# Attention on one Trainium2 core: the engine loops run over pairs of query blocks, and the q rows stand in a ring of two blocks

## The reference

```python
q = (x @ Wq.T).reshape(N, S, H, hd).transpose(0, 2, 1, 3)   # k, v alike; N 4, S 2048, H 16, hd 32
energy = jnp.einsum('nhqd,nhkd->nhqk', q, k)
attn = jax.nn.softmax(energy / jnp.sqrt(hd), axis=3)
out = jnp.einsum('nhql,nhld->nhqd', attn, v)
x = _layernorm(x + out.transpose(0, 2, 1, 3).reshape(N, S, D))
y = clip(einsum('bsi,oi->bso', x, sign(weights)) * scale + bias, -100, 100)
x = _layernorm(x + y)
```

## Time and profile before

| | us |
|---|---|
| median of 3 runs (lowest to highest) | 3060.59 (3056.12 to 3070.12) |
| the profiled execution | 3055.99 |
| its span | 3053.8 |
| PE busy / DVE busy / ACT busy in the span | 2816.3 / 2320.8 / 2300.6 |
| idle time of PE ahead of its score matmuls (line 637) | 194.4 |
| ACT_TABLE_LOAD in attention (line 764) | 16 of 1.283 each |

### The profile page before, as it was taken

The page is one execution under the profiler, slowest core; times in us unless marked ns, Lnnn a source line. Parts: engine busy times, 40 slices in busy tenths (PEclk is TensorE's granted clock), DMA queues, the critical chain, the costliest instruction groups (busy, mean ns, idle before and its releaser), DMA issues.

```text
span 3053.8 us, 79127 instructions
## 1 busy us (share of the span) xinstructions
PE 2816.3 (92%) x29276; PEld 1339.6 (44%) x29276; DVE 2320.8 (76%) x2050; ACT 2300.6 (75%) x2789; POOL 342.5 (11%) x342
## 2 busy tenths in 40 slices
PE   8999999898989889898989889898988989997998
PEld 7888888632323223232323223332322323335887
DVE  4443344398979788887979788887978888896998
ACT  4333333398979788887979788997978888894665
POOL 0000000100000000000000000000000000003665
PEclk9999999899999999999999999999999999997999
DMA  5454544457666575656666584756657565655563
GB/s 197 169 188 165 181 176 175 170 124 155 128 140 131 122 162 111 141 112 148 127 136 137 115 168 106 154 121 143 133 121 159 114 146 112 148 114 161 205 205 128
DMA packets 223651, 446.51 MB, mean 146 GB/s; under 512 B 15442, under 2 KB 130130, under 8 KB 198868
## 3 DMA queue, kind: packets, MB, share of 16 engines
q0 software_dynamic: 27504, 200.29, 33.9%
q1 hardware_dynamic: 186596, 224.71, 23.6%
q10 hardware_dynamic: 9216, 16.78, 1.4%
HBM read 123.47 MB, written 117.96 MB: 79 GB/s over the span
## 4 chain that ended last, share of the span: by engine, by line
PE 60%; issue 11%; ACT 5%; DVE 2%; ACTq 0%; DMA 0%; POOL 0%; DVEq 0%; SPq 0%; POOLq 0%
PE banks L637 27%; PE banks L666 24%; PE banks L1008 6%; ACT probs L764 5%; PE banks L683 1%; DVE partial L818 1%; DVE partial L821 1%; PE banks L997 1%; PE banks L990 1%; PE banks L1004 0%; DMA total<-partial 0%; POOL score_rows L587 0%; PE banks L991 0%; ACTq L756 0%; ACT y L1026 0%
## 5 line engine op out<-in xcount | busy, mean ns | idle before, releaser
L764 ACT ACTIVATE probs<-banks 128x1024 f32<-128x1024 f32 x2048 | 1892.6, 1162 | 154.5 <-PE banks L637 153.0
L637 PE MATMUL banks<-score_rows 97*32 97x512 f16 x16384 | 1170.2, 392 | 194.4 <-ACT probs L764 111.8
L666 PE MATMUL banks<-probs,v_keys 128*32 128x512 f32 x8192 | 1093.3, 610 | 5.8 <-ACT probs L764 4.5
L637 PEld LDWEIGHTS banks<-score_rows 97*32 97x32 f16 x16384 | 379.8, 97 | 1243.6 <-ACT probs L764 681.9
L821 DVE TENSOR_TENSOR partial<-partial,probs 128x2048 f32<-128x2048 f32 x384 | 879.6, 2291 | 19.0 <-ACT probs L764 6.4
L818 DVE TENSOR_TENSOR partial<-probs 128x2048 f32<-128x2048 f32 x192 | 440.1, 2292 | 163.4 <-ACT probs L764 160.6
L606 POOL DMA_DIRECT2D total<-partial x191 | 164.5, 861 | 1986.6 <-DVE partial L821 1030.2
L666 PEld LDWEIGHTS banks<-probs,v_keys 128*32 128x32 f32 x8192 | 253.0, 114 | 234.6 <-issue 29.3
L821 DVE TENSOR_TENSOR total<-total,probs 128x2048 f32<-128x2048 f32 x128 | 292.7, 2287 | 10.6 <-ACT probs L764 8.5
L348 DVE TENSOR_TENSOR qk_lo<-banks,qk_hi 128x512 f16<-128x512 f32 x128 | 88.5, 691 | 239.2 <-ACT qk_hi L292 239.2
L818 DVE TENSOR_TENSOR total<-probs 128x2048 f32<-128x2048 f32 x64 | 146.4, 2288 | 140.6 <-ACT probs L764 136.5
(11 more groups left out here) (94 smaller groups left out, 2159.1 us busy)
## 6 DMA issues: line engine op xcount, KB each, us to landing
total<-partial POOLq DMA_DIRECT2D x191, 1024.0 KB, 8.0
x_in<-in_L_attn_x SPq DMA_DIRECT2D x17, 1024.0 KB, 7.3
scratch_q_raw<-qk_raw SPq DMA_DIRECT2D x16, 1024.0 KB, 5.5
scratch_k_raw<-qk_raw SPq DMA_DIRECT2D x16, 1024.0 KB, 5.6
scratch_v<-v_out SPq DMA_DIRECT2D x16, 1024.0 KB, 5.0
score_rows<-scratch_q_hi SPq DMA_DIRECT2D x128, 128.0 KB, 6.4
score_rows<-scratch_k_hi SPq DMA_DIRECT2D x128, 128.0 KB, 3.8
v_keys<-scratch_v SPq DMA_DIRECT2D x64, 256.0 KB, 5.5
```

Of the source, the lines that this page charges most:

```text
L637: last = nc.tensor.matmul(scores_of(unit)[part, i, :], k_rows[:, h, keys], q_rows[:, h, qb * BLK:(qb + 1) * BLK], start=True, stop=True)
L666: last = nc.tensor.matmul(banks[rows, out_bank(qb), :], v_keys[:, kt, rows], probs[:, kt % P_RING, h, :], start=(kt == 0), stop=(kt == KT ...
L764: nc.scalar.activation(probs[:, kt % P_RING, heads, :], scores_of(qb * UNITS + u), ACT.Exp, scale=SCALE / GAIN ** 2).then_inc(a_prob, 1)
```

## The change

The loops of PE, ACT and DVE run over 32 pairs of query blocks, not over 16 items, and write out two blocks (`par` is 0 or 1), not four. The last pair is written out behind PE's loop, and the first ahead of DVE's. `score_rows` is split into `q_pair`, two blocks of q, and `k_item`, an item's k. Block n of q goes to slot n % 2, and SP loads block n+2 when the scores of block n are done. Since 64 units don't divide by 3 slots, the last unit of a pair takes slot 1, and the credit of `a_prob` is 4. SP increments `a_order` ahead of some DMAs.

```diff
-    rows16 = sb("score_rows", [P, 2, G, S], FP16)
-    q_rows, k_rows = rows16[0:KROWS, 0], rows16[0:KROWS, 1]
+    q_pair = sb("q_pair", [P, 2 * G * BLK], FP16)
+    k_item = sb("k_item", [P, G * S], FP16)
+    q_rows = q_pair[0:KROWS].rearrange("p (b h t) -> p b h t", b=2, h=G)
+    k_rows = k_item[0:KROWS].rearrange("p (h t) -> p h t", h=G)
...
+    PAIRS = ITEMS * QB // 2
+    LAST_PAIR = PAIRS - 1
+    CREDIT = SLOTS + 1
+
+    def slot_of(unit):
+
+        return 1 if unit == 2 * UNITS - 1 else unit % SLOTS
 
     def scores_of(unit):
 
-        return banks[:, 2 * (unit % SLOTS):2 * (unit % SLOTS) + 2, :]
+        return banks[:, 2 * slot_of(unit):2 * slot_of(unit) + 2, :]
...
-            for c in range(1, QB):
-                load_q(0, c)
+            load_q(0, 1)
             with sp.Fori(0, LAST) as it:
...
                     sp.wait_ge(a_score, st * UNITS + UNITS)
-                    load_q(ahead, qb)
+                    sp.sem_inc(a_order, 1)
+                    load_q(it if qb < 2 else ahead, (qb + 2) % QB)
...
+            for qb in range(2):
+                sp.wait_ge(a_score, (LAST * QB + qb + 1) * UNITS)
+                load_q(LAST, qb + 2)
...
-        def fast_scores(it, qb, kt):
+        def fast_scores(pair, par, kt):
             if kt == 0:
-                pe.wait_ge(a_q[qb], it * FIRST_Q + FIRST_Q)
-            if qb == 0 and kt % TPB == 0:
-                pe.wait_ge(a_k[kt // TPB], it * FIRST_K + FIRST_K)
+                pe.wait_ge(a_q[par], pair * FIRST_Q + FIRST_Q)
+            if par == 0 and kt % TPB == 0:
+                pe.wait_ge(a_k[kt // TPB], pair // 2 * FIRST_K + FIRST_K)
             for half in range(2):
-                unit = qb * UNITS + 2 * kt + half
-
-                pe.wait_ge(a_prob, it * ITEM_UNITS + slot_before(unit) + 1 + SLOTS)
+                unit = par * UNITS + 2 * kt + half
+
+                pe.wait_ge(a_prob, pair * 2 * UNITS + slot_before(unit) + 1 + CREDIT)
...
-        def item(scores, it):
-
-            steps(scores, it, 0, range(HEAD, KT))
-            for qb in range(1, QB):
-                steps(scores, it, qb, range(KT))
-            if it is not LAST:
-                steps(scores, it + 1, 0, range(HEAD))
-            denominators(it, QB - 1)
+        def two_blocks(scores, pair):
+
+            steps(scores, pair, 0, range(HEAD, KT))
+            steps(scores, pair, 1, range(KT))
+            if pair is not LAST_PAIR:
+                steps(scores, pair + 1, 0, range(HEAD))
+            denominators(pair, 1)
...
-            with pe.Fori(0, ITEMS - 1) as it:
-                item(scores, it)
-            item(scores, LAST)
+            with pe.Fori(0, LAST_PAIR) as pair:
+                two_blocks(scores, pair)
+            two_blocks(scores, LAST_PAIR)
...
-        def item(it):
-            for qb in range(QB):
-                st = it * QB + qb
+        with act.Fori(0, PAIRS) as pair:
+            for par in range(2):
+                st = pair * 2 + par
...
-        nc.vector.tensor_scalar(q_rows[3 * HD:KROWS], k_rows[3 * HD:KROWS], 0.0, shift[3 * HD:KROWS], ALU.mult, ALU.add).then_inc(a_shift, 1)
+        nc.vector.tensor_scalar(q_pair[3 * HD:KROWS], k_item[3 * HD:KROWS, 0:2 * G * BLK], 0.0, shift[3 * HD:KROWS],
+                                ALU.mult, ALU.add).then_inc(a_shift, 1)
...
-        item(0, True)
-        with dve.Fori(1, ITEMS) as it:
-            item(it, False)
+        two_blocks(0, True)
+        with dve.Fori(1, PAIRS) as pair:
+            two_blocks(pair, False)
```

More of the change, by code:

```diff
@@ L406, in attend @@
     out_sb, den_sb = wf_scaled[:, 0:2, :], wf_scaled[:, 2:4, :]
-    a_q = [sem(f"a_q{c}") for c in range(QB)]
+    a_q = [sem(f"a_q{c}") for c in range(2)]
     a_k = [sem(f"a_k{c}") for c in range(QB)]
@@ L438, in attend @@
     UNITS = 2 * KT
-    ITEM_UNITS = QB * UNITS
+    PAIRS = ITEMS * QB // 2
     LAST = ITEMS - 1
+    LAST_PAIR = PAIRS - 1
     HEAD = DEN_TILE + 1
@@ L443, in attend, with out_bank @@
     FIRST_K = 48
+    CREDIT = SLOTS + 1
+    def slot_of(unit):
+        return 1 if unit == 2 * UNITS - 1 else unit % SLOTS
     def scores_of(unit):
-        return banks[:, 2 * (unit % SLOTS):2 * (unit % SLOTS) + 2, :]
+        return banks[:, 2 * slot_of(unit):2 * slot_of(unit) + 2, :]
     def slot_before(unit):
-        return unit - SLOTS if unit >= SLOTS else max(v for v in range(ITEM_UNITS) if v % SLOTS == unit) - ITEM_UNITS
-    def out_bank(qb):
-        return 2 * SLOTS + qb % 2
+        units = range(2 * UNITS)
+        return max(v for v in [*[u - 2 * UNITS for u in units], *range(unit)] if slot_of(v % (2 * UNITS)) == slot_of(unit))
+    def out_bank(par):
+        return 2 * SLOTS + par
     v_src = dram["v"].rearrange("(n b) (t p) (g d) -> n g b p t d", n=N, p=P, g=NG)
@@ L636, in fast_scores, with exact_scores @@
                         keys = slice(kt * P + HD * c, kt * P + HD * c + HD)
-                        last = nc.tensor.matmul(scores_of(unit)[part, i, :], k_rows[:, h, keys],
-                                                q_rows[:, h, qb * BLK:(qb + 1) * BLK], start=True, stop=True)
+                        last = nc.tensor.matmul(scores_of(unit)[part, i, :], k_rows[:, h, keys], q_rows[:, par, h, :],
+                                                start=True, stop=True)
                 last.then_inc(a_score, 1)
-        def exact_scores(it, qb, kt):
-            st = it * QB + qb
+        def exact_scores(pair, par, kt):
+            st = pair * 2 + par
             if kt == 0:
@@ L655, in exact_scores, with values @@
                 last.then_inc(a_score, 1)
[L657 to L661, removed]
+        def values(pair, par, kt):
+            st = pair * 2 + par
+            if par == 0 and kt % TPB == 0:
+                pe.wait_ge(a_v[kt // TPB], pair // 2 * 16 + 16)
+            pe.wait_ge(a_prob, st * UNITS + 2 * kt + 2 + CREDIT)
             if kt == 0:
@@ L665, in values, with denominators @@
                 rows = slice(HD * h, HD * h + HD)
-                last = nc.tensor.matmul(banks[rows, out_bank(qb), :], v_keys[:, kt, rows], probs[:, kt % P_RING, h, :],
+                last = nc.tensor.matmul(banks[rows, out_bank(par), :], v_keys[:, kt, rows], probs[:, kt % P_RING, h, :],
                                         start=(kt == 0), stop=(kt == KT - 1))
             last.then_inc(a_pv, 1)
[L670 to L673, removed]
+        def denominators(pair, par):
+            st = pair * 2 + par
+            parts = [total[:, par]]
+            if pair is LAST_PAIR and par == 1:
                 pe.wait_ge(a_merged, (st + 2) * (GROUPS - 1) - 1)
@@ L682, in denominators, with steps, all_blocks @@
                     rows = slice(HD * h, HD * h + HD)
-                    last = nc.tensor.matmul(banks[rows, out_bank(qb), :], ones[:], part[:, h, :],
+                    last = nc.tensor.matmul(banks[rows, out_bank(par), :], ones[:], part[:, h, :],
                                             start=(part is parts[0]), stop=(part is parts[-1]))
             last.then_inc(a_den, 1)
-        def steps(scores, it, qb, tiles):
+        def steps(scores, pair, par, tiles):
             for kt in tiles:
                 if kt + LAG < KT:
[L691 to L699, removed]
-        def item(scores, it):
-            steps(scores, it, 0, range(HEAD, KT))
-            for qb in range(1, QB):
-                steps(scores, it, qb, range(KT))
-            if it is not LAST:
-                steps(scores, it + 1, 0, range(HEAD))
-            denominators(it, QB - 1)
-        def all_items(scores):
+                    scores(pair, par, kt + LAG)
+                elif par == 0:
+                    scores(pair, 1, kt + LAG - KT)
+                elif pair is not LAST_PAIR:
+                    scores(pair + 1, 0, kt + LAG - KT)
+                values(pair, par, kt)
+                if kt == DEN_TILE and par == 1:
+                    denominators(pair, 0)
+        def two_blocks(scores, pair):
[4 more added lines that the diff above has]
+            denominators(pair, 1)
+        def all_blocks(scores):
             for kt in range(LAG):
@@ L736, in _ @@
             pe.wait_ge(m_ones, 1)
-            all_items(exact_scores)
+            all_blocks(exact_scores)
         with pe.Else():
@@ L802, in copy_den, with two_blocks @@
             nc.vector.tensor_copy(den_sb[:, parity, :], banks[:, out_bank(parity), :]).then_inc(a_dout, 1)
-        def item(it, first):
-            for qb in range(QB):
-                st = it * QB + qb
+        def two_blocks(pair, first):
+            for par in range(2):
+                st = pair * 2 + par
                 for kt in range(KT):
@@ L810, in item @@
                         continue
-                    into = total[:, qb % 2] if g == 0 else partial[:, g - 1]
-                    dve.wait_ge(a_prob, st * UNITS + 2 * kt + 2 + SLOTS)
+                    into = total[:, par] if g == 0 else partial[:, g - 1]
```

(1 more changed line is left out.)

36 lines of the change are left out of this document (17 added, 19 removed).

## The result

| | before | changed |
|---|---|---|
| median, us (lowest to highest) | 3060.31 (3056.12 to 3070.12) | 3202.29 (3196.93 to 3204.43) |
| ratio to before, 95% interval | | 1.0457 (1.0428 to 1.0485) |

What follows compares the result with a forecast made beforehand. It blamed instruction fetches at PE's and ACT's loop jumps. Attention: 64 x 29.69 = 1900.2, + 46.5 + 6 + 1.2 = 1953.9 against 2149.4 us; with the start 196.7 less, 2859.3 profiled, 2864 median, range 2840 to 2900.

Steps and rivals of the forecast that it cites:

- part 2: PE's loop over pairs: about 1,680 instructions, 7 packets touched and 1 ahead, held in an inferred store of 8.
- I take 0: PE's jump back in its loop over pairs: no cost if held, between bounds of 0 and 6.9 us per jump.
- rival B: PE's loop not held: 31 jumps at 6.9 us, 22 us for packets crossed late, 3100 us in all; chance 0.13.
- ACT's loop is held: ACT's loop over pairs: some 195 instructions, three packets at most with one ahead; 31 jumps at 1.5 us, 46.5.
- The held sum: Whole kernel with both loops held: attention 1953.9 us, median 2864, within 2840 to 2900; chance 0.72.
- The 6 for the PSUM slots: 64 units don't divide by 3 slots, so units wait for a later exp: 6 us, between 0 and 29.
- the distance from profiled execution to median: The profiled execution, 3056.0 us, lies 4.6 under the median of the runs; this takes 2859.3 to 2864.
- The q ring at 0: SP's q loads with one block of lead, 29.7 us: no cost, between 0 and 1 us per block (64).
- Rival D: Loops held, but half clock behind table loads, or merges or DVE, set the pace: 2900 to 2930 us; chance 0.10.
- Rival C: Neither PE's nor ACT's loop held, twice the jumps at the old price, 31 x 17.9: 3365 us; chance 0.03.
- Rival E: The gap is a fixed price of the jump, not the fetch, or q is late: within 0.5% of before; chance 0.02.
- q8 with some 270 packets or more and PE gaps of 5 us twice per item is B: Sign on PE's instruction queue and timeline that PE's loop is not held; right would be under 60 packets.

Runs made afterwards that it cites:

- e1: The changed kernel with 40 never-run semaphore increments ahead of the exact path in PE's stream: 2857.45 us, ratio to before 0.9339.
- e5: The changed kernel with 8 never-run semaphore increments ahead of the exact path in PE's stream: 2857.69 us, ratio to before 0.9350.
- e6: The changed kernel with 7 never-run semaphore increments ahead of the exact path in PE's stream: 3210.50 us, ratio to before 1.0504.
- e12: The changed kernel with POOL's merges moving 8 of 128 partitions, 64 KB in place of 1 MB: 3072.97 us, ratio to before 1.0056.
- e11: The kernel before with 63 never-run semaphore increments, so PE's loop starts 4 instructions ahead of a packet's edge, not 67: 3055.60 us, ratio 1.0005.
- e9: The changed kernel with 40 never-run increments and PE's loop left over items, ACT's over pairs: 3011.53 us, ratio to before 0.9857.
- e7: The changed kernel with 230 never-run semaphore increments ahead of the exact path in PE's stream: 3176.61 us, ratio to before 1.0393.
- e4: The changed kernel with 140 never-run semaphore increments ahead of the exact path in PE's stream: 2859.80 us, ratio to before 0.9347.
- e8: The changed kernel with 40 never-run increments and one 128x1 exp ahead of ACT's loop, taking the table load out: 2816.99 us, ratio 0.9217.

## Why the prediction was wrong

- **The failing step is part 2, "I work out a start 7 instructions behind a packet's edge".** The loop starts 8 ahead of one. The size of the body (1,680 against 1,665), the packets of 256 instructions and the 8 that are held were all right (e1, e5, e6). What was off by 15 is the sum of the code ahead of the loop, with a margin of 7: 13 in the body of the exact loop, 2 in where the edge lies. So the term "I take 0" for PE's jump measured 11.5 us. I had written that margin down under rival B and still gave the rival 0.13: a count by hand of several thousand instructions had no claim to be right to 7.
- **The price in rival B was too small.** It had 3100 for 3202. Against the held loop of e1 the changed kernel loses 3202.3 - 2857.5 = 344.8, or 11.5 us for each of the 30 jumps; I had 6.9 for each of 31, and 22 in all for late packets. The first packet holds 8 instructions, so that two fetches follow one another, and both run beside a merge. The gaps are 8.5 of the 11.5. The other 3.0 I did not take apart; in the changed kernel the clock is at 0.50 for 307 us of attention, in e1 for none, and a slower PE is the likely part. The merge is 4.3 of the 11.5 (e12). The second gap is of the same kind as the one that e11 added to the kernel before, at 4.5 us per jump.
- **That ACT's loop is held was right.** 14 packets on q14, 16.9 us of idle time ahead of 32 table loads (0.53 each; I had said under 0.5). Each of its 31 jumps costs 1.77 us over the pitch; I had 1.5, between bounds of 1.41 and 3.1, which is 8 us too little over 31 jumps.
- **The held sum came out, in part by luck.** It gave 2864, and the loop with its start moved took 2857.45. For attention it gave 1953.9 us; in e1, from ACT's first exp of the stage to the end of its last, it is 2557.07 + 5.61 - 608.35 = 1954.3. But two terms in it are off and offset each other. The jumps cost 1.76 each, 54.5 us and not 46.5. The 6 for the PSUM slots cost nothing: the units in question, 63 and those after it, show nothing beyond ACT's own jump. The 6.5 us between forecast and median lie outside attention: 3.8 are the distance from profiled execution to median, taken as 4.6 and here 0.8. The forecast failed by the start alone.

```profile
608.35 5.60 ACT L777 ACTIVATE probs<-banks 128x1024 f32<-128x1024 f32 x6
...
2557.07 5.61 ACT L777 ACTIVATE probs<-banks 128x1024 f32<-128x1024 f32 x6 [0.26 <-PE banks L649]
```

- **The q ring at 0 was right**: in e1 the idle time of PE ahead of the scores has no DMA among its releasers, only ACT 40.7 and DVE 11.7 us.
- **Rival D was rightly small.** In e1 the clock stays at 1.00 through the table load, and a block takes 29.69 us (939.13 to the next at 968.82), as in the earlier trace rows. In the changed kernel the clock does fall, but behind gaps of 9 us, as a consequence of B.
- **Rival C is answered by q14.** Rival E is refuted by e5 and e6: the price goes with the fetches.

Of what the text had named as signs, "q8 with some 270 packets or more and PE gaps of 5 us twice per item is B" was met, with 291 and four gaps per item.

## What to carry to other kernels

A loop that nearly fills an engine's instruction store is a matter of where it starts, not only of its length: count the packets that it touches from the built program, or better, move it by a few never-run instructions and look at the packets of the instruction queue. Price a missed jump from a trace in which the same DMAs run beside it, for here a jump with two fetches cost 11.5 us with 1 MB merges and 7.2 with 64 KB ones. And count how far the start lies ahead of an edge: with 67, 50, 34 and 8 instructions ahead the second gap had a median of 0, 1.5, 3.0 and 3.7 us (the kernel before, e9, e7, the changed kernel). Where a forecast has a margin of a few instructions in thousands, its chance should be that of the margin, not that of the mechanism.

## What was not expected of the hardware

- One instruction that is never executed moved the time from 3210.50 to 2857.69 us.
- A loop that touches 8 packets was held when it ended 5 instructions into the last (e4), and not when it ended 95, 121 or 128 into it (e7, the changed kernel, e6).
- A fetch of instructions starts later beside data, and isn't slower: with merges of 1 MB PE's first packet after the branch started after 4.3 us and took 0.95, with 64 KB after 1.0 and took 1.0 (medians of 30 jumps). The two gaps had means of 4.8 and 3.7 us, and 1.9 and 2.7.
- Behind the end of a packet the first matmul came after 1.6 us (medians of the kernel before, the changed kernel and e12 alike).
- Two losses offset one another in e11: PE's jumps cost 63 us more and ACT's 59 less, where the merge had got further by the time of ACT's jump. The median alone would have said that nothing happened.
- Open: why the jump of ACT without a table load still costs 0.49 us (e8), what holds the start of a fetch back beside a merge, what the 3.0 us per jump beyond the gaps are, and at which instruction of a packet the next is asked for.
